# Attention stage: where in TensorE's order the softmax maximum is subtracted

## The reference, cut to what matters

```python
q = (t @ Wq.T + bq)            # tokens;  k, v: 64 clips x 12 frames, 2 heads of 64
logits  = einsum('avhd,bthd->abhvt', k, q) / sqrt(64)
weights = softmax(logits, axis=3)              # over the 12 frames of one clip
attn    = einsum('avhd,abhvt->abhtd', v, weights)
attn    = attn.mean(axis=0)                    # over the 64 clips
o       = attn @ Wo.T + bo
```

## Time and profile before

| | |
|---|---|
| time, 3 runs | 2370.89 us median (2363.86 to 2371.24) |
| profiled execution, first to last instruction | 2375.5 us |
| main runs and products of the attention stage in it | about 1142 to 1620 us |
| TensorE matmul busy, whole span | 2056.8 us (87%) |
| VectorE busy, whole span | 1627.6 us (69%) |
| ScalarE busy, whole span | 1076.7 us (45%) |
| GpSimd busy, whole span | 607.4 us (26%) |

### The profile page before, as it was taken

The page is one execution under the profiler, slowest core; times in us unless marked ns, Lnnn a source line. Parts: engine busy times, 40 slices in busy tenths (PEclk is TensorE's granted clock), DMA queues, the critical chain, the costliest instruction groups (busy, mean ns, idle before and its releaser), DMA issues. The chain is left out here.

```text
span 2375.5 us, 54798 instructions
## 1 busy us (share of the span) xinstructions
PE 2056.8 (87%) x20986; PEld 1814.0 (76%) x20986; DVE 1627.6 (69%) x4183; ACT 1076.7 (45%) x2698; POOL 607.4 (26%) x650
## 2 busy tenths in 40 slices
PE   6699989998626785786899999995999999999998
PEld 5587777887624685776677777774999999999998
DVE  4755665554743553556699999996777777777774
ACT  4433333332514453453566666662444444444443
POOL 0002222200054425430233333334122122222220
PEclk9699999999757897898999999997999999999999
DMA  8100110100311101100000000000000000000000
GB/s 179 39 1 11 14 13 11 13 4 1 104 47 34 31 18 42 28 24 1 2 3 3 3 3 3 3 3 1 8 8 7 13 7 7 13 7 7 13 7 14
DMA packets 80355, 44.51 MB, mean 19 GB/s; under 512 B 45800, under 2 KB 74024, under 8 KB 79752
## 3 DMA queue, kind: packets, MB, share of 16 engines
q1 hardware_dynamic: 74248, 29.53, 5.5%
q0 software_dynamic: 5888, 12.07, 1.9%
HBM read 27.20 MB, written 14.38 MB: 18 GB/s over the span
## 5 line engine op out<-in xcount | busy, mean ns | idle before, releaser
L2104 ACT ACTIVATE w<-banks,b 128x384 f32<-128x384 f32 (+1 forms) x512 | 259.6, 573 | 393.0 <-PE banks L2178 393.0
L2160 PE MATMUL banks<-w,w 128*128 128x128 f32 (+1 forms) x3072 | 364.1, 275 | 0.0
L2160 PEld LDWEIGHTS banks<-w,w 128*128 128x128 f32 (+1 forms) x3072 | 350.4, 189 | 9.1 <-issue 8.7
L1688 PE MATMUL banks<-qT,w 64*64 64x128 f32 x4608 | 272.2, 271 | 3.2 <-ACT eb L1640 2.4
L1696 PE MATMUL banks<-eb,w 64*64 64x128 f32 x4608 | 272.4, 271 | 0.2 <-DVE eb L1595 0.2
L1688 PEld LDWEIGHTS banks<-qT,w 64*64 64x64 f32 x4608 | 249.3, 133 | 16.7 <-DVE eb L1595 2.2
L1660 POOL TENSOR_TENSOR t<-eb 128x768 f32<-128x768 f32 x96 | 174.6, 1819 | 309.4 <-ACT eb L1640 299.5
L1696 PEld LDWEIGHTS banks<-eb,w 64*64 64x64 f32 x4608 | 249.2, 133 | 0.9 <-DVE eb L1595 0.8
L2001 DVE SCALAR_TENSOR_TENSOR h<-banks,t_wt,h 128x128 f32 (+3 forms) x672 | 183.6, 342 | 83.1 <-PE banks L2160 79.6
L1237 POOL DMA_INDIRECT xg<-xs,rowu x184 | 178.7, 971 | 154.3 <-PE banks L1388 95.1
L1595 DVE TENSOR_TENSOR eb<-eb,rd 128x1536 f32<-128x1536 f32 x96 | 208.5, 2172 | 2.1 <-ACT rd L1649 2.1
(11 more groups left out here) (300 smaller groups left out, 4360.4 us busy)
## 6 DMA issues: line engine op xcount, KB each, us to landing
out<-h SPq DMA_DIRECT2D x16, 320.0 KB
xs<-r_xl SPq DMA_DIRECT2D x16, 192.0 KB, 2.9
h<-in_xT SPq DMA_DIRECT2D x4, 750.0 KB, 15.5
h<-in_xT SPq DMA_DIRECT2D x4, 749.0 KB, 18.5
xg<-xs,rowu POOLq DMA_INDIRECT x184
xs<-r_xl SPq DMA_DIRECT2D x16, 128.0 KB
blocks<-NT SPq DMA_DIRECT2D x24, 48.0 KB, 1.9
D<-blocks SPq DMA_DIRECT2D x24, 48.0 KB, 2.0
```

The costliest lines, as they stand in the source:

```text
L1688: last = nc.tensor.matmul(lbanks(n)[place(n, hd), v, :], k.Kt[half(hd), v, :], qT[half(hd), n // NC % 2, (n % NC) * P:(n % NC + 1) * P], s ...
L2104: nc.scalar.activation(gb[u % 2][:, f, s * GW:s * GW + NFREE[s]], k.ps[:, order.bank(n), 0:NFREE[s]], ACT.Relu, bias=k.b1_1[:, 2 * e + f:2 ...
L2160: last = nc.tensor.matmul(k.psf[0:n, o:o + P], gb[u % 2][:, f, c * P:c * P + n], k.w2_1[:, 2 * e + f, :], start=(f == 0), stop=(f == 1))
```

## The change

The three products with the identity are no longer behind the main run and the preparation of queries, but inside the main run, ahead of frame 8 of 12 (`v == 2 * FB`). Their wait for `m_ready` moves with them. In step 96, which has no logits but values, they are inside the value products in the same way. No instruction is added or taken out, and the programs of the other engines are the same.

```diff
+                def shift(e):
+                    pe.wait_ge(m_ready, e + 1)
+                    for s in range(3):
+                        nc.tensor.matmul(lbanks(e)[:, s * FB:(s + 1) * FB, :], k.identb[:, :],
+                                         nm[:, e % 2, None, :].to_broadcast([P, FB, P]), start=False, stop=True,
+                                         skip_group_check=True).then_inc(shifted, 1)
+
...
                     for v in range(FR):
+                        if v == 2 * FB and 1 <= n <= NCH:
+                            shift(n - 1)
                         if logits:
                             if v % FB == 0 and n >= 2:
                                 pe.wait_ge(e_ready, 3 * (n - 2) + v // FB + 1)
...
                             nt.turn(pe, *now, 7)
-                    if 1 <= n <= NCH:
-                        pe.wait_ge(m_ready, n)
-                        for s in range(3):
-                            nc.tensor.matmul(lbanks(n - 1)[:, s * FB:(s + 1) * FB, :], k.identb[:, :],
-                                             nm[:, (n - 1) % 2, None, :].to_broadcast([P, FB, P]), start=False, stop=True,
-                                             skip_group_check=True).then_inc(shifted, 1)
                     if 0 <= o < NCH:
                         pe.wait_ge(a_ready, o + 1)
```

## The result

The changed kernel takes 2438.86 us (median of 4 runs, 2435.45 to 2447.07), the kernel before 2367.38 (4 runs, 2362.64 to 2371.24). The ratio is 1.0309, with a 95% interval of 1.0285 to 1.0333: slower by 67 to 79 us. Forecast were 74 us more and 2445 us.

What follows compares the result with a forecast made beforehand. The prediction took TensorE's program to set the step, with VectorE full partly because its multiply is slowed. Terms of 54.6 + 15.1 + 3 + 1.5 = 74 us more gave 2445 us, range 2412 to 2470.

Steps and rivals of the forecast that it cites:

- Who waits for the shift: ScalarE: only its exponentials wait for the shift, with 0.0 us idle before them, so an earlier shift brings none forward.
- Slot steps: The 60 turn and query steps: the shift, hidden beside ScalarE's copy, now stands on the chain; 0.91 us each, 54.6 us.
- a sign: Profile of the changed kernel: output product in slot steps waits 0.9 to 1.2 us for ScalarE's copy instead of 0.2 to 0.4.
- The switches: TensorE changing between quarters and whole array: two pairs a step instead of one, 0.26 us for a pair.
- Plain steps: The other 36 steps: the next main run waits for the first, later exponential; 0.42 us each, 15.1 us.
- The wait for the maximum: Shift ahead of frame 8 waits for VectorE's maximum: 0.2 us in each of 16 pairs of plain steps, 3 us.
- if VectorE is free: Condition under which the maximum takes until 5.54 us from its step's start, leaving 1.04 us in a plain step.
- The end: Step 96: the values stand behind the last shift and its wait, so the last exponentials start about 1.5 us later.
- the switches are free: Rival: on TensorE only the products count; 45 us more, 2416 us; chance 0.18.
- VectorE becomes the bound: Rival: its multiply falls together with GpSimd's whole addition; 122 us more, 2493 us as the far end; chance 0.12.
- No change: Rival: VectorE sets the pace, so TensorE's 0.91 us more is slack; time stays at 2371 us; chance 0.04.
- faster: Rival: VectorE's multiply no longer lies beside GpSimd's addition; 40 us less, 2331 us; chance 0.06.

Runs made afterwards that it cites:

- The kernel with the early exponentials: Changed kernel with ScalarE's three exponentials put ahead of its copy `aT`, and one wait added: 2431.57 us, ratio 1.0232 against the kernel before.
- the kernel with plain steps alone: Kernel before with the shift ahead of frame 8 only in the 36 plain steps, behind the main run in turn and query steps: 2282.90 us, ratio 1.0079.
- The kernel with this half of the change alone: Kernel before with the shift ahead of frame 8 only in the 60 turn and query steps: 2325.81 us, ratio 1.0265.
- the one-column product: Kernel before, shift still late, plus one added whole-array product with a single column ahead of frame 8: 2292.05 us, ratio 1.0104.
- leaving them out in quarters: Changed kernel with each shift product as two 64x64 products on the main run's quarters: 2324.64 us, ratio 1.0256 against the kernel before.
- the two frames: Changed kernel with the shift ahead of frame 4 or frame 11 instead of 8: 2475.05 us (ratio 1.0415) and 2443.67 us (1.0278).
- the kernel with the shorter bias product: Kernel before, shift late, with the output bias as one bf16 product instead of two fp32 passes: 2367.96 us, ratio 0.9964.

## Why the prediction was right

*Who waits for the shift.* It held: 0.0 us of idle time before the exponentials in both kernels, and 158.6 us once they could wait for it. One detail was finer than I had it. In a plain step before, the first exponential started 0.27 us after the copy `aT` began, in the changed kernel 0.18 after. So the shift did hold it back by 0.09 us. The kernel with the early exponentials bears this out: there they wait for the shift and start 0.43 us after its start, as they do in a plain step before (1286.82 to 1287.25). The 0.09 us show in no idle time, since the exponential starts before the copy ahead of it has ended (1295.38 against 1295.20 + 0.28).

*Slot steps.* 0.91 us forecast. Measured 0.91 in query steps and in the turn steps behind them; in the turn steps behind plain ones 1.14, of which 0.32 is the wait for the maximum; a wait of 0.09 us for bank 7, which they had before, is gone, as in the kernel with plain steps alone. By 60 steps the 0.91 are 55 us, as forecast. The kernel with this half of the change alone is 59 us slower (57 to 63 by the interval); its parts add up to 63: 55, 9 of waits for the maximum, and 1 less for the wait that is gone. The output product's wait for the copy, 0.8 us in a slot step, is a little less than the 0.9 to 1.2 that I had named as a sign.

*The switches.* 0.26 us from gaps in the trace; 0.26 again in the changed kernel, 0.27 by the one-column product, 0.27 by leaving them out in quarters. The Trainium skill's rule in "TensorEngine Tiling (Array Packing)", Key Properties, that a change of the tiling mode drains TensorE, agrees. The runs give the time between the starts around a change; how much of it is draining and how much the loading of new weights they don't separate.

*Plain steps.* 0.42 forecast, 0.40 measured, but two errors met. TensorE goes on 0.13 us after the exponential is done (4.04 + 0.60 = 4.64, start at 4.77), not 0.06; and the exponential is 0.83 later, not 0.91, for the reason above. TensorE's own time in a plain step grew by 0.16 and not by 0.26, as the kernel with the early exponentials shows (4.53 us): before, the output product began 0.75 us after the shift began, 0.10 more than its three products need, and that gap is gone: the output product now follows the main run directly, 0.22 us after the start of its last group.

*The wait for the maximum.* 3 us forecast, 8 us measured by the two frames: the term that was mis-sized. I had it in the second plain step alone, 0.2 us; it is 0.17 there and 0.32 in the turn step behind it, which I had left out, though the delay in a plain step is handed on to the next. The step that failed is "if VectorE is free": the maximum was to start when the logits are done, 3.79 us after the step's start, and to be through at 5.54, with 1.04 us left. VectorE isn't free then. Its timeline for the plain step above (start 1291.34), and the shift that waits for this maximum:

```profile
1292.43 2.93 DVE L1595 TENSOR_TENSOR eb<-eb,rd 128x1536 f32<-128x1536 f32 x1 [0.48 <-ACT rd L1649]
...
1295.87 0.59 DVE L1587 TENSOR_REDUCE den<-t 128x128 f32<-128x384 f32 x1
1296.38 1.75 DVE L1591 TENSOR_REDUCE nm<-banks 128x128 bf16<-128x1536 f32 x1
```

```profile
1298.18 0.82 PE L1672 MATMUL banks<-nm,identb 128*128 128x512 bf16 x3
```

The maximum stands behind the stretched multiply and two short instructions, starts at 5.04 and is through at 6.79. The next main run starts at 4.77 and reaches frame 8 at 1.91, that is 6.68: no room is left, and the shift waits until 2.07 (1296.11 to 1298.18). That 3 us and 8 us lie so near each other is in part luck. VectorE's multiply went to 2.71 us in the mean, where some 2.78 was estimated.

*The end.* 1.5 us forecast. The last exponential ends 1.2 us later after the start of step 96 than before (5.94 us, not 4.77).

*The sum.* 74 us forecast, 71 by the medians, 76 by the stage in the profiles.

*The rivals.* That the switches are free (45 us): out. That VectorE becomes the bound: not here, its share fell to 95%, and the waits for its maximum cost 8 us and not 122. But in the plain steps of the kernel with the shorter bias product it did. No change and faster: out, and with the exponentials first neither came.

What stays open: why the multiply's stretch is always the overlap less some 0.14 us. No run changed GpSimd's addition itself.

## What to carry to other kernels

Before a step is moved earlier on an engine, look for idle time of its consumer that the step ends. If there is none, the consumer stands behind something else in its own program, and the move can only delay what is put behind the step. And look at what the step lay beside: a product that fills the time in which another engine copies costs nothing there and its full price anywhere else. On TensorE a product of the whole array inside a run on quarters cost 0.27 us here, even with a single column.

## What the runs showed of the hardware

- A pair of changes between 64x64 quarters and the whole array costs 0.26 to 0.27 us here, with three products of 512 columns between them or with one of a single column. With bf16 products on quarters in the same place it isn't paid.
- Two products of 512 columns on two diagonal quarters run side by side (a pair every 0.21 to 0.22 us, like one product of the whole array), and logit products on the other quarters start between them. TensorE's timeline of the kernel with the shift in quarters:

```profile
1192.12 0.28 PE L1700 MATMUL banks<-qT,w 64*64 64x128 f32 x2
1192.14 0.38 PE L1673 MATMUL banks<-nm,identb 64*64 64x512 bf16 x2
1192.23 0.28 PE L1700 MATMUL banks<-qT,w 64*64 64x128 f32 x2
1192.35 0.38 PE L1673 MATMUL banks<-nm,identb 64*64 64x512 bf16 x2
```

- VectorE's multiply of two SBUF inputs, 1.75 us alone, took 2.93 us where GpSimd's addition went on for its first 1.3 us; the maximum out of PSUM took 1.75 us beside it in every case.
